# In block 0's first stage, the first two products of a slab move ahead of the next slab's first unit of combinations

## What is computed

```python
s = silu(xn @ w_gate.T)                      # 2048 x 2752
# of each token's 2752 values, the 1376 smallest in size are set to 0
s = (s with those zeroed) * (xn @ w_up.T)
s = s @ w_down.T                             # branch A, back to 1024
g = silu((silu(xn @ W_gate.T) * (xn @ W_up.T)) @ W_down.T)   # branch B
out = x + s * g
```

## Time and profile before

| | us |
|---|---|
| median of 3 runs | 2768.76 |
| lowest and highest | 2768.42, 2770.05 |
| the profiled execution | 2768.99 |
| its span in the profile | 2767.2 |
| TensorE busy in it | 2745.4 |
| VectorE, ScalarE, GpSimd busy | 2298.5, 1350.6, 408.4 |

### The profile page before, as it was taken

The page is one execution under the profiler, slowest core; times in us unless marked ns, Lnnn a source line. Parts: engine busy times, 40 slices in busy tenths (PEclk is TensorE's granted clock), DMA queues, the critical chain, the costliest instruction groups (busy, mean ns, idle before and its releaser), DMA issues.

```text
span 2767.2 us, 31398 instructions
## 1 busy us (share of the span) xinstructions
PE 2745.4 (99%) x12204; PEld 2275.1 (82%) x12204; DVE 2298.5 (83%) x3002; ACT 1350.6 (49%) x1386; POOL 408.4 (15%) x185
## 2 busy tenths in 40 slices
PE   9999999999999999999999999999999999999999
PEld 7878888878788888888878888888887888888887
DVE  6776989999976798998986688999898667999971
ACT  4235988332445477731145457771115546776110
POOL 5565443074400000000020000000011000000000
PEclk9999999999999999999999999999999999999999
DMA  6898888579766555556666655555666664555564
GB/s 234 313 337 286 294 288 278 211 265 362 256 195 192 179 192 197 192 190 223 245 205 191 193 179 197 189 191 197 243 220 205 193 196 180 188 193 198 191 232 169
DMA packets 135097, 614.28 MB, mean 222 GB/s; under 512 B 12752, under 2 KB 12752, under 8 KB 89168
## 3 DMA queue, kind: packets, MB, share of 16 engines
q1 hardware_dynamic: 134992, 612.94, 63.2%
HBM read 492.31 MB, written 120.59 MB: 221 GB/s over the span
## 4 chain that ended last, share of the span: by engine, by line
PE 88%; DVE 8%; DMA 2%; issue 1%; ACT 0%; POOL 0%; SPq 0%; DVEq 0%; POOLq 0%; ACTq 0%
PE ps L634 27%; PE ps L854 19%; PE ps L883 11%; PE ps L882 11%; PE ps L884 11%; PE ps L784 2%; PE ps L785 2%; PE ps L787 2%; DMA w_raw<-w_a 1%; DVE prods L1364 1%; DVE key_buf L1635 1%; DVE hid_ring L1407 1%; DVE xnT L1355 1%; DVE key_buf L1643 1%; DVE ranks L1605 1%
## 5 line engine op out<-in xcount | busy, mean ns | idle before, releaser
L634 PE MATMUL ps<-w_split,hid_ring 128*128 128x512 f32 x4096 | 933.7, 390 | 3.7 <-DVE hid_ring L1407 2.1
L634 PEld LDWEIGHTS ps<-w_split,hid_ring 128*128 128x128 f32 x4096 | 769.1, 188 | 167.2 <-issue 5.4
L1390 DVE TENSOR_SCALAR_CACHE_REDUCE ranks<-key_buf,cand 128x2752 int16<-128x2752 f32 x248 | 762.8, 3076 | 5.8
L968 ACT ACTIVATE signs_row<-key_buf,cand 128x2752 bf16<-128x2752 f32 x248 | 642.2, 2590 | 191.7 <-DVE cand L1399 182.2
L884 PE MATMUL ps<-xnT,w_split 128*128 128x512 f32 x1376 | 535.3, 389 | 0.0
L883 PE MATMUL ps<-xnT,w_split 128*128 128x512 f32 x1376 | 535.3, 389 | 0.0
L882 PE MATMUL ps<-xnT,w_split 128*128 128x512 f32 x1376 | 535.3, 389 | 0.0
L1216 POOL TENSOR_TENSOR w_split<-w_raw,w_split 128x1024 fp32r<-128x1024 f32 (+3 forms) x142 | 309.7, 2195 | 354.3 <-ACT w_split L935 134.6
L884 PEld LDWEIGHTS ps<-xnT,w_split 128*128 128x128 f32 x1376 | 258.3, 188 | 53.8
L882 PEld LDWEIGHTS ps<-xnT,w_split 128*128 128x128 f32 x1376 | 258.3, 188 | 53.7
L883 PEld LDWEIGHTS ps<-xnT,w_split 128*128 128x128 f32 x1376 | 258.3, 188 | 53.2
(11 more groups left out here) (146 smaller groups left out, 2884.6 us busy)
## 6 DMA issues: line engine op xcount, KB each, us to landing
w_split<-split SPq DMA_DIRECT2D x272, 1024.0 KB, 4.8
split<-w_split SPq DMA_DIRECT2D x72, 1024.0 KB, 6.7
w_raw<-w_a SPq DMA_DIRECT2D x97, 512.0 KB, 3.7
w_raw<-t_dram SPq DMA_DIRECT2D x81, 512.0 KB, 3.3
w_raw<-w_b SPq DMA_DIRECT2D x42, 512.0 KB, 4.8
t_dram<-t_buf SPq DMA_DIRECT2D x20, 1024.0 KB, 8.5
w_extra_raw<-t_dram SPq DMA_DIRECT2D x39, 512.0 KB, 3.3
w_extra_raw<-w_a SPq DMA_DIRECT2D x33, 512.0 KB, 3.6
```

Source lines behind the costliest of these rows:

```text
L634: ins = pe.matmul(ps[:, 2 * t + half, :], h, w[:, half * TB:(half + 1) * TB], start=(first and n == 0), stop=last and stop)
L968: act.activation(signs_row[:, :], keys[:, t, :], ACT.Sign, bias=cand_f[:, t:t + 1], scale=-1.0, accum_out=counts[:, t:t + 1]).then_inc(act ...
L1390: dve.tensor_scalar(ranks[:, :], keys[:, t, :], cand_f[:, t:t + 1], 0.0, ALU.is_lt, ALU.add, accum_out=counts[:, t:t + 1]).then_inc(sel_st ...
```

## The change

`a_prods` takes a range of row tiles. In block 0, DVE first does the products of row tiles 0 and 1 of slab s, then the unit (s + 1, 0), then the products of row tiles 2 and 3. For the last slab, which has no unit behind it, nothing changes but the call.

```diff
-                def a_prods(s, wide):
+                def a_prods(s, wide, tiles=range(NT)):
                     cols = slice(s * SLAB, s * SLAB + wide)
-                    for t in range(NT):
+                    for t in tiles:
                         dve.wait_ge(a_silu, (s * NT if b == 0 else rest_events(b, NT)) + (t + 1))
...
                     for s in range(NS):
+                        a_prods(s, SLAB, range(STAGE))
                         if s + 1 < NS:
                             t_unit((s + 1, 0))
-                        a_prods(s, SLAB)
+                        a_prods(s, SLAB, range(STAGE, NT))
                         if s + 1 < NS:
                             t_unit((s + 1, 1))
                         a_keys(s, SLAB)
```

## The result

| | before | changed |
|---|---|---|
| median of 3 runs, us | 2768.76 | 2785.52 |
| lowest and highest | 2768.42, 2770.05 | 2784.17, 2785.56 |
| span of the profiled execution | 2767.2 | 2783.8 |

The changed kernel is 16.8 us slower; the ratio is 1.0054 with a 95% interval of 1.0040 to 1.0068. The forecast was 2781.8, with a range from 2776.5 to 2786.5.

What follows compares the result with a forecast made beforehand. TensorE, busy for 99% of the span, was taken as the bound. Slab starts cost 14.2 us less 3.56 removed, +10.7, and lateness further down +2.3: 2782.0 profiled, 2781.8 by the median, range 2776.5 to 2786.5.

Steps and rivals of the forecast that it cites:

- The first wait: Starts of slabs 1 to 4: TensorE waits for GpSimd's low part until T + 2.32; 2.43 us lost, 3.0 at slab 2.
- T: Time the next slab's first matmul would start if unheld: start of the last L787 row plus 2 x 0.23 us.
- The second wait: After the starts of slabs 1 and 4: row tile 2's matmul waits for its product behind the unit, 1.96 us each.
- two waits for L1423: Predicted sign: TensorE waits about 1.8 us for products, 2.7 us after the starts of slabs 1 and 4.
- Further down the slab: Slabs 1 and 4: later units and loads make low parts of tiles 12 and 36 late by 1.2 and 1.1 us.
- Behind stage A: After stage A: nothing known takes the delay back, since VectorE's search starts when stage A ends; no added term.

Runs made afterwards that it cites:

- e2: Changed kernel plus 14 transposes of the identity filling TensorE's pause at the starts of slabs 1 to 4; 2783.92 us against 2785.52 of the changed kernel.
- e4: Kernel before with the new order only at the end of slab 2; 2773.44 us, 3.65 more than before.
- e1: Changed kernel with the unit split: L1446 and the copy ahead of the first two products, its second half behind them; 2767.39 us, 2.4 less than before.
- e3: Changed kernel with all four products ahead of the unit; 2795.13 us, ratio 1.0094 to before.
- e5: e1 with GpSimd's low_stage behind low of the same place and SyncE's spill one load later; 2766.72 us, ratio 0.9986 to before.
- e7: Changed kernel with only the product of row tile 0 ahead of the unit, the others behind; 2784.98 us.
- e6: Kernel before, all products behind the unit, with low_stage behind low and SyncE's spill one load later; 2764.00 us, 5.9 less than before.

## Why the prediction was right, and where it fell short

The direction and the mechanism were right: the wait for banks went, and the low part of each slab's first tile took its place. The size was short by 3.7 us. The terms that fell short are the clock, which the sum left out, and ACT's late roundings at the ends of slabs 1 and 3. By places, in us lost on TensorE, slow matmuls included (from the starts of its matmuls, against 0.227 us each):

| place | before | forecast | measured |
|---|---|---|---|
| start of slab 1 | 1.27 | 4.39 | 4.3 = 2.41 + 1.87 slow |
| start of slab 2 | 0 | 3.0 | 5.0 = 3.3 + 1.7 slow |
| start of slab 3 | 0.43 | 2.43 | 2.5 |
| start of slab 4 | 1.86 | 4.39 | 4.95 = 3.1 + 1.85 slow |
| tiles 12 and 36 | 0 | 1.2 + 1.1 | 1.2 + 1.3 |
| tiles 20 and 21 | 1.9 | 1.9 | 1.6 |

- *The first wait* was forecast at 2.32 and measured at 2.41, 3.31, 2.40 and 3.09. Those at slabs 2 and 4 are longer because ACT rounded a late tile ahead of the silus. I had that for slab 2 alone; at the end of slab 3 the two silus ran to 199.88, at T - 1.35. That makes 0.7 more than forecast at slab 4; at slab 2 it was 0.4 more, since tile 17 came later still (101.78, T - 3.2).
- *The second wait* (1.96, twice) isn't in the changed profile, and my check on it, two waits for L1423, failed. The step was right, as e2 shows: 1.79 and 0.11 for the pause, at both places, once the clock is kept up. In the changed kernel TensorE came to row tile 2 later by itself, since its matmuls were slow: at slab 1 its product ends near 62.74 (62.05 + 0.69), and the matmul starts at 62.79, hardly later than it would have.
- *The missing term* is the clock. It cost 1.7 us or so at each of three starts. At slabs 1 and 4 it took the place of the second wait (1.96), so the sum there came out nearly right by luck, as two errors cancel; at slab 2, which had no second wait, its 1.6 were simply missing.
- *Further down the slab* (+2.3) was right: 2.5 at tiles 12 and 36, against 1.2 + 1.1. SP's chain ran as read: the spill at 60.88 and the load of tile 11 at 61.73.
- *Behind stage A* I had nothing. The table's sum is 20.9 against 5.5, so 15.4 us where the sum of the prediction had 13.0. The line for tiles 20 and 21 is the least firm in it, since the wait at tile 20 differs between profiles with nothing changed ahead of it (e4). VectorE's first product with the down projection at the end of block 0 is 15.2 us later (728.07 and 743.31), and so is TensorE's start into block 1. The last 1.5 us come right behind that start. The kernel before, TensorE's timeline:

```profile
729.35 5.74 PE L854 MATMUL ps<-w_extra,xnT 128*128 128x512 f32 x24 [1.99 <-DVE hid_buf L1707]
```

The changed kernel:

```profile
744.59 7.21 PE L854 MATMUL ps<-w_extra,xnT 128*128 128x512 f32 x24 [3.54 <-DVE hid_buf L1708]
```

The 24 matmuls last 7.21 instead of 5.74 us. The granted clock, in a stretch of block 0's last stage of the kernel before:

```profile
606.00:616.00 10.00, 7.96 (x28) 6.42 (x29) 5.43 (x6) 8.15 (x11) 3.94 (x3) 0.83 0.68 283
```

In the same stretch of the changed kernel, and at its start into block 1:

```profile
621.00:631.00 10.00, 7.90 (x36) 6.36 (x35) 5.15 (x7) 8.36 (x11) 3.86 (x3) 1.00 0.79 308
...
744.60:748.50 3.90, 3.90 (x11) 3.09 (x12) 3.90 (x4) 0.00 (x0) 3.82 (x2) 0.59 0.16 63
```

Before, the clock fell behind this pause, in the last stage of block 0:

```profile
608.04 7.33 PE L634 MATMUL ps<-w_split,hid_ring 128*128 128x512 f32 x24 [2.08 <-DVE hid_ring L1407]
```

TensorE waited for VectorE at the end of that stage anyway. In the changed kernel the clock didn't fall there. TensorE reached the end of the block 1.5 us sooner relative to VectorE, waited 3.54 instead of 1.99 us, and the clock fell there, where the next 24 matmuls pay for it. The profile of e1, no slower than before, shows the second pattern too (a pause of 3.58 us), as do those of e3, e4, e5 and e7, and that of e6 the first (2.07), so it isn't tied to the change as far as these runs show. That of e2 has both falls, behind pauses of 2.24 and 3.18 us. What decides between them is open, and so is how much of the longer pause comes from the missing fall. Some 1.5 us of any comparison of single profiles can come from it.

My sums were too hopeful by 1.2 us in e1, and by 2.1 in e5 counted from e1. For e5 the rows offer a reason: with the second half of the unit behind the products, `low` of the slab's second tile starts at T + 0.8 (57.91) instead of T - 2.2 as in e6 (54.53), and the next units come later too, so that other tiles come just late. e5 lost 3.1 us at tiles 13, 36 and 37, where e6 lost nothing, and differs from e6 only in the split of the unit and in the two products ahead of its second half. For e1 the waits in slab 2 are a part of it, and tile 20's need not be the edit's.

## What to carry to other kernels

Before an instruction is moved ahead in an in-order queue, look at who waits for what it jumps over: here a short copy was the head of a chain (copy, subtraction, matmul) with a slack of 3 us, and it was put behind an instruction that can't start until 1.9 us before the deadline. Where an instruction on the path is long beyond its kind (2.87 us instead of 0.69), look at what stretches it before changing its own engine's order: moving the `low_stage` and its spill gave 5.9 us here, and the reorder cost 16.8. A pause that a change puts on TensorE is to be priced with the slow matmuls that may follow it (a pause of 2.25 us was followed by 1.9 us of them here), and those may in turn hide the next wait.

## What the runs showed of the hardware that I had not expected

- The clock fell in or behind pauses of 2.25, 2.92 and 3.15 us in the changed kernel, and cost 1.7 to 1.9 us each time, restarts included; behind pauses of 2.24 and 2.10 us in the same execution it didn't, yet behind one of 2.24 us in e4 it did.
- Over the nine profiles, from stage A's start to the start of block 1, the clock fell in or behind each of the 15 pauses of 2.8 us or more, 5 of the 14 pauses of 2.06 to 2.30 us, and none of those up to 1.99 us. No pause lay between 2.30 and 2.84.
- In the pauses of 5 us in e3 the clock fell before the pause was over, and still cost about as much behind it: 2.0 us in slow matmuls at slab 1, restart included, against 1.9 in the changed kernel. The granted clock of the pause at slab 1 and of the stretch behind it in e3:

```profile
56.00:61.00 5.00, 0.20 (x1) 0.00 (x0) 4.23 (x5) 1.54 (x2) 2.42 (x2) 0.75 0.00 0
61.00:65.50 4.50, 4.34 (x11) 3.46 (x12) 4.47 (x5) 0.00 (x0) 3.15 (x2) 0.52 0.23 95
```

- With fourteen transposes of 128 x 128 (1.7 us of work) in the pauses of e2, the clock stayed up at all three places where it had fallen in the changed kernel.
